# Graph-transformer layer: transposes, masks and scores of two thirds of the attention pair by pair in one TensorE array mode, ScalarE with fewer masks and more copies

## The reference, cut to what matters

```python
scores = einsum('ehd,ehd->eh', q[origin], k[destination]) * SCALE
ws = scores * edge_weights
e = exp(ws - segment_max(ws, origin)[origin])
att = e / (segment_sum(e, origin)[origin] + 1e-16)
values = segment_sum(att[:, :, None] * v[destination], origin)
values = (values @ W1 + b1) @ W2 + b2
```

## Time and profile before

| | us |
|---|---|
| median of 3 runs (1079.01 to 1079.73) | 1079.44 |
| profiled execution | 1079.38 |
| its span, first to last instruction | 1077.5 |
| around the span | 1.9 |
| PE busy in the span | 737.6 |
| VectorE (DVE) busy | 544.0 |
| ScalarE (ACT) busy | 397.4 |
| attention, first scores to the end | 673 to 1077.5 |

### The profile page before, as it was taken

How to read it: one execution, slowest core, us unless ns; L and a number is a source line. 1 busy time by engine, 2 the same in 40 slices (tenths; PEclk the granted TensorE clock), 3 DMA queues, 4 the chain that set the end, 5 groups by cost and what they waited for, 6 DMA issues and landing times.

```text
span 1077.5 us, 13741 instructions
## 1 busy us (share of the span) xinstructions
PE 737.6 (68%) x4498; PEld 436.4 (41%) x4537; DVE 544.0 (50%) x1269; ACT 397.4 (37%) x943; POOL 392.7 (36%) x401
## 2 busy tenths in 40 slices
PE   7744510494332211115999999999999999999996
PEld 4321100241001011003544454576766667767773
DVE  4601400482000110200532473888889999999998
ACT  2300001020000000001313020689989998877773
POOL 2677577477777776562572000000000000000002
PEclk9956655696555555556999999999999999999998
DMA  9788866536500000002400021444444444443323
GB/s 323 270 292 302 281 239 212 179 112 219 193 23 3 23 3 22 22 3 79 153 2 1 1 79 78 149 185 172 158 157 157 161 164 167 150 140 137 137 69 96
DMA packets 71115, 143.12 MB, mean 133 GB/s; under 512 B 22565, under 2 KB 57137, under 8 KB 67079
## 3 DMA queue, kind: packets, MB, share of 16 engines
q1 hardware_dynamic: 48884, 120.06, 30.7%
q10 hardware_dynamic: 8464, 15.84, 4.2%
q0 software_dynamic: 13696, 6.33, 3.1%
HBM read 77.47 MB, written 64.80 MB: 132 GB/s over the span
## 4 chain that ended last, share of the span: by engine, by line
PE 50%; another core or an unknown queue 20%; issue 20%; DVE 6%; ACT 2%; DMA 2%; ACTq 1%; DVEq 0%; POOLq 0%
PE bank L1092 11%; PE bank L1319 9%; PE bank L1364 7%; PE bank L1342 7%; PE bank L1077 6%; PE bank L1388 3%; PE bank L1326 2%; DVE AR L1841 1%; PE bank L1370 1%; DMA AR<-in_L_mix_bp_dram 1%; DVE QMN L1451 1%; DVE QMN L1450 1%; PE bank L1112 1%; DMA AR<-kv_rows,xd 1%
## 5 line engine op out<-in xcount | busy, mean ns | idle before, releaser
L630 POOL DMA_INDIRECT w_tab<-pay,idx x330 | 326.5, 989 | 160.0 <-issue 116.1
L1077 PE MATMUL bank<-AR 128*128 128x512 f32 (+1 forms) x288 | 130.9, 587 | 122.7 <-issue 102.8
L705 POOL DMA_INDIRECT AR<-kv_rows,xd x10 | 10.5, 1051 | 445.4 <-PE bank L1364 331.6
L1092 PE MATMUL bank<-AR 128*128 128x512 f32 (+1 forms) x240 | 128.6, 666 | 62.4 <-issue 62.4
L1077 PEld LDWEIGHTS bank<-AR 128*128 128x128 f32 x288 | 62.3, 222 | 180.3 <-issue 156.3
L1541 DVE TENSOR_TENSOR V<-bank,bias_row 128x512 f32<-128x512 f32 (+1 forms) x10 | 6.9, 691 | 250.0 <-remote 153.5
L912 ACT ACTIVATE AR<-AR,nmx 128x512 f32<-128x512 f32 (+1 forms) x180 | 118.5, 662 | 20.6 <-DVE nmx L1855 20.5
L1841 DVE CUSTOM_DVE_ANT_0 AR<-bank,AR,MX 128x512 f32<-128x512 f32 (+1 forms) x120 | 114.9, 986 | 8.6 <-remote 7.6
L1319 PE MATMUL bank<-KT,QT 64*128 64x512 f32 (+1 forms) x480 | 108.6, 568 | 4.0 <-ACT bank L920 3.7
L1092 PEld LDWEIGHTS bank<-AR 128*128 128x128 f32 (+1 forms) x240 | 48.3, 205 | 133.5 <-issue 133.0
L1364 PE MATMUL bank<-AR,V 128*64 128x128 f32 (+1 forms) x1520 | 101.9, 274 | 0.2 <-ACT AR L927 0.2
(11 more groups left out here) (272 smaller groups left out, 1013.2 us busy)
## 6 DMA issues: line engine op xcount, KB each, us to landing
w_tab<-ztile SPq DMA_DIRECT2D x20, 2280.0 KB
AR<-w_tab SPq DMA_DIRECT2D x20, 2048.0 KB, 7.4
AR<-w_tab SPq DMA_DIRECT2D x10, 1344.0 KB, 6.2
w_tab<-ztile SPq DMA_DIRECT2D x3, 1800.0 KB
w_tab<-pay,idx POOLq DMA_INDIRECT x330
w_tab<-ztile SPq DMA_DIRECT2D x2, 1700.0 KB
kv_rows<-AR ACTq DMA_DIRECT2D x9, 256.0 KB
kv_rows<-V ACTq DMA_DIRECT2D x9, 256.0 KB
```

The source lines that it names most:

```text
L630: pool.indirect_dma_start(out=w_tab, out_offset=bass.IndirectOffsetOnAxis(ap=idx[:, k, j:j + 1], axis=0), in_=pay[:, k % RING, j, :], in_o ...
L1077: last = mm(b[:, 0:n], w[:, k, m * P:(m + 1) * P], src_t(k), start=(k == 0), stop=(k == KC - 1))
L1092: last = mm(b[0:r, :], src_t(k)[:, 0:r], w[:, k, :], start=(k == 0), stop=(k == KC - 1))
```

## The change

In groups 0 and 1 and in the even steps of group 2 (`paired`), TensorE works pair by pair: scores of pair u, first half of its masks, first halves of the transposes of pair u-2, second half of the masks, second halves of the transposes. Masks and transposes are split by rows of the array, 64 at a time, head 0 in one half of the rows while head 1 is in the other, and then the other way round. Between first and second halves TensorE waits for its own first ones (`s_mh`, `s_th`). `factor`, `inverse` and the first `loser_k` are split the same way there. The order of `USES` follows. ScalarE lays only the masks of pair 2 (and in group 2 head 1 of pair 3) and copies head 1 of pairs 0 and 2, of pairs 0, 1 and 2, and of pair 2 in the three groups. ScalarE's and VectorE's orders in groups 0 and 1 are rewritten pair by pair. The values stay as they are, and so do the odd steps of group 2.

```diff
-ODD_ON_ACT = ((2,), (1, 2), ())
-OVER_MASK = (((3, 1), (1, 1), (2, 0), (2, 1)), ((3, 1), (1, 1), (2, 0), (2, 1)), ((2, 0), (2, 1), (3, 1), (0, 0), (1, 0)))
+ODD_ON_ACT = ((0, 2), (0, 1, 2), (2,))
+OVER_MASK = (((2, 0), (2, 1)), ((2, 0), (2, 1)), ((2, 0), (2, 1), (3, 1)))
...
+def paired(d):
+    return d < 4 * NT or (d < ND and d % 2 == 0)
+def half(j, n):
+    return slice(64 * j, min(64 * j + 64, n))
...
 for _d in range(ND + 4):
     _w, _q = _d // 2, _d % 2
+    if paired(_d):
+        USES += [("s", 2 * _d, 0), ("s", 2 * _d, 1)]
+        if _q == 1 and NT <= _w - 1:
+            USES += [("f", _w - 1)]
+        if _d:
+            USES += [("t", 2 * _d - 2, 0), ("t", 2 * _d - 2, 1)]
+        USES += [("s", 2 * _d + 1, 0), ("s", 2 * _d + 1, 1)]
+        if _q == 1 and _w + 1 == 2 * NT:
+            USES += [("l", _w + 1)]
+        if 2 * NT <= _w - 2:
+            USES += [("r", _w - 2)]
+        if _d:
+            USES += [("t", 2 * _d - 1, 0), ("t", 2 * _d - 1, 1)]
+        continue
...
 ...
+                if w < 2 * NT:
+                    if d:
+                        pairs(2 * d - 2)
+                    if q == 0 and NT <= w - 1:
+                        change(w - 1)
+                    if q == 0 and 2 <= w <= NT + 1:
+                        keep(w - 2)
+                    exps(2 * d)
+                    if q == 0:
+                        for u, hh in lay_order(d):
+                            lay_mask(u, hh)
...
+                    if d:
+                        pairs(2 * d - 1)
+                    exps(2 * d + 1)
...
 ...
+            def mask_half(u, part):
+                w, n = u // 4, GROUPS[u // 4 // NT][1]
+                bare = [hh for hh in range(2) if not laid(u, hh)]
+                if bare and part:
+                    pe.wait_ge(s_mh, mh.n)
...
+                for hh in bare:
+                    rows = half((hh + part) % 2, P)
+                    last = mm(use(("s", u, hh))[:, 0:n], identb[rows, :], pen[w % 2][rows, 0:n], start=False, stop=(part == 1))
...
+            def turn_halves(u, part):
+                g, r = u // 4 // NT, rows_of(u // 4 % NT)
+                bl = blocks(g)
+                if part == 0:
+                    for hh in range(2):
+                        pe.wait_ge(s_exp, 2 * u + hh + 1)
+                        free(pe, ("t", u, hh))
+                for i, (a, rws, _) in enumerate(bl):
+                    for hh in range(2):
+                        rows = half((hh + part) % 2, r)
+                        last = mm(use(("t", u, hh))[0:rws, i * P + rows.start:i * P + rows.stop], ws[g][u % 4][hh][rows, a:a + rws], ident[rows, rows],
+                                  start=(part == 0 and i == 0), stop=(part == 1 and i == len(bl) - 1), is_transpose=True)
...
+            def pair_step(d, i):
+                w, q = d // 2, d % 2
+                u, older = 2 * d + i, 2 * d - 2 + i
...
+                pair_scores(u)
+                mask_half(u, 0)
+                if fac:
+                    factor_half(w - 1, 0)
...
+                if inv:
+                    inverse_half(w - 2, 0)
+                if d:
+                    turn_halves(older, 0)
+                mask_half(u, 1)
+                pe.wait_ge(s_th, th.n)
+                if fac:
+                    factor_half(w - 1, 1)
...
+                if inv:
+                    inverse_half(w - 2, 1)
+                if d:
+                    turn_halves(older, 1)
...
 ...
+                if w < 2 * NT:
+                    if q == 0 and NT <= w - 1:
+                        change(w - 1)
+                    if q == 0 and NT <= w - 2:
+                        merged(w - 2)
+                    weighted(2 * d, 0)
+                    weighted(2 * d, 1)
+                    early = q == 1 and w + 1 == 2 * NT
+                    if early:
+                        rescaled(w - 1)
+                    if d:
+                        odd_of(2 * d - 2)
+                    shift_of(2 * d)
+                    weighted(2 * d + 1, 0)
+                    weighted(2 * d + 1, 1)
+                    if q == 1 and NT <= w - 1 and not early:
+                        rescaled(w - 1)
+                    shift_of(2 * d + 1)
+                    if q == 1:
+                        mask(w + 1)
...
+                    if d:
+                        odd_of(2 * d - 1)
+                    if q == 0 and NT <= w - 1:
+                        denominators(w - 1)
```

More of the change, by code:

```diff
@@ L94, in lay_order @@
     else:
-        order = ((0, 0), (0, 1), (1, 1)) if late else ((1, 1), (0, 0), (0, 1))
+        order = ((0, 0), (0, 1), (1, 1)) if late else ((0, 0), (0, 1))
     return [(2 * d + 2 + i, hh) for i, hh in order if d + 1 < ND and laid(2 * d + 2 + i, hh)]
@@ L993, in _ @@
                             lay_mask(u, hh)
-                    if late:
-                        pairs(2 * d - 1)
+                    pairs(2 * d - 1)
                     exps(2 * d)
@@ L1326, in scores, with pair_scores @@
                         mm(use(("s", u, hh))[:, 0:n], identb[:, :], pen[w % 2][:, 0:n], start=False, stop=True).then_inc(s_s[i], 1)
+            mh, th = Count(pe, s_mh), Count(pe, s_th)
+            def pair_scores(u):
+                w, p = u // 4, u % 4
+                g, c = w // NT, w % NT
+                d0, n = GROUPS[g]
+                over = [laid(u, hh) for hh in range(2)]
+                if g == 2 and p == 0:
+                    gone(pe, ("l", w))
+                if u in (1, 2):
+                    banks_left((2 * u - 2, 2 * u - 1))
+                for hh in range(2):
+                    if over[hh]:
+                        pe.wait_ge(s_laid, LAID_OF[u, hh] + 1)
+                    else:
+                        free(pe, ("s", u, hh))
+                for hh in range(2):
+                    last = mm(use(("s", u, hh))[:, 0:n], QT[64 * hh:64 * hh + 64, p, c * P:(c + 1) * P], KT[64 * hh:64 * hh + 64, p, d0:d0 + n],
+                              start=not over[hh], stop=over[hh], skip_group_check=over[hh])
+                    if over[hh]:
+                        last.then_inc(s_s[2 * (u % 2) + hh], 1)
@@ new lines, in factor_half @@
+            def factor_half(w, part):
+                if part == 0:
+                    pe.wait_ge(s_fo, w - NT + 1)
+                    free(pe, ("f", w))
+                rows = half(part, P)
+                for p in range(KC):
+                    last = mm(use(("f", w))[:, p * P + rows.start:p * P + rows.stop], fo[rows, p * P:(p + 1) * P], ident[rows, rows],
+                              start=(part == 0 and p == 0), stop=(part == 1 and p == KC - 1), is_transpose=True)
+                if part:
+                    last.then_inc(s_fp, 1)
+                else:
+                    th.inc(last)
@@ new lines, in inverse_half @@
+            def inverse_half(w, part):
+                if part == 0:
+                    pe.wait_ge(s_rb, w - 2 * NT + 1)
+                    free(pe, ("r", w))
+                rows = half(part, P)
+                for p in range(KC):
+                    last = mm(use(("r", w))[:, p * P + rows.start:p * P + rows.stop], te[rows, p * P:(p + 1) * P], ident[rows, rows],
+                              start=(part == 0 and p == 0), stop=(part == 1 and p == KC - 1), is_transpose=True)
+                if part:
+                    last.then_inc(s_rp, 1)
+                else:
+                    th.inc(last)
@@ new lines, in loser_half @@
+            def loser_half(w, part):
+                c = w - 2 * NT
+                if part == 0:
+                    pe.wait_ge(s_kvx[c % 3], 16 * (c // 3 + 1))
+                    free(pe, ("l", w))
+                rows = half(part, X)
+                for k in range(KC):
+                    last = mm(use(("l", w))[:, k * X + rows.start:k * X + rows.stop], KVx[c % 3][rows, k * P:(k + 1) * P], ident[rows, rows],
+                              start=(part == 0 and k == 0), stop=(part == 1 and k == KC - 1), is_transpose=True)
+                if part:
+                    last.then_inc(s_kxp, 1)
+                else:
+                    th.inc(last)
@@ L1415, in _ @@
                     ffn(w - 2)
-                if q == 1 and 2 * NT <= w + 1 < NW:
+                if q == 1 and 2 * NT <= w + 1 < NW and not paired(d):
                     loser_k(w + 1)
-                if 1 <= d <= ND:
+                if d <= ND and not paired(d):
                     transposes(d - 1)
```

53 lines of the change are left out of this document (38 added, 15 removed).

## The result

The changed kernel takes 1106.84 us (median of 4 runs, 1104.39 to 1109.63), the kernel before 1079.22 beside it: ratio **1.0263** [1.0232, 1.0294], slower.

What follows compares the result with a forecast made beforehand. TensorE was taken as the bound, with an order across three engines running just beside it. Group terms of +1.5, +12.5 and +5.9 us sum to +19.9 on 1079.38, so 1099 us, range 1074 to 1114.

Steps and rivals of the forecast that it cites:

- main case: Orders across engines and bank waits in all three groups outweigh TensorE's saving: +19.9 us, 1099 us, chance 64%.
- only group 0's chain holds: Rival: bank waits of groups 1 and 2 are covered by something misread; 1081 to 1086 us, chance 10%.
- Group 0: Even step 6.91 us by laid masks behind two exponentials, odd 5.6; tile 12.5 against 12.4, +1.5 us over ten tiles.
- Group 1: Laid masks, transposes' bank and `rescaled`'s bank hold the steps: tile 14.45 us against 13.0, +12.5 us in all.
- Group 2: Even steps: pair 3's transposes wait for the bank of pair 0's second scores, +0.74 us each, +5.9 us in all.
- The bounds: Ranges around each group's sum: -4 to +7 us in group 0, +6 to +17 in group 1, 0 to +9 in group 2.
- TensorE's own work: Group 0: scores, masks, half transposes, values and waits add up to 11.4 us a tile against 12.4.
- PE busy falls by 15 us or more: Sign over the whole kernel: TensorE's busy time falls that much while the span grows.
- Price of a round: Half transposes on TensorE: 0.06 us for two heads side by side, 0.24 for a group of four rounds.
- TensorE's wait for itself: Between first and second halves: 0.06 us behind a mask half, 0.31 where nothing is between, as in pair 2.
- the saving comes through: Rival: group 0 goes at 11.4 us, group 1 at 11.7 + 0.3; 1060 us, with half of it 1070; chance 17%.
- rival of halves that don't overlap: Rival: two heads' half transposes run one after the other, four rounds 0.48 us; 19 us more, 1118 us; chance 9%.

Runs made afterwards that it cites:

- e1: Changed kernel with ScalarE laying pair 2's masks ahead of pair 0's exponentials in groups 0 and 1: 722.96 us, 1.0154 of the kernel before.
- e2: Changed kernel with `rescaled` moved ahead of the second pair's products on VectorE in all of group 1: 732.16 us, 1.0283 of the kernel before.
- e3: Changed kernel with group 2 put back as in the kernel before, its laid masks too: 731.3 us, 1.028 of the kernel before.
- e7: Changed kernel with the edits of e1, e2 and e3, and VectorE's next-tile mask behind an odd step's first shift: 1077.7 us, 0.9981 of the kernel before.
- e10: e7 with, in group 1, VectorE's denominators moved to the odd step and all transposed heads copied by ScalarE: 1069.7 us, 0.9953 of the kernel before.

## Why the prediction was right, and where it was off

- **The main case held**, in its mechanism and its sign. The three waits it named are there: laid masks behind two exponentials in groups 0 and 1 (1.0 us each), `rescaled` whose bank is the next tile's (0.8), the transposes of pair 3 behind pair 0's bank in group 2 (0.65). e1, e2 and e3 take away one each: 14.2, 5.4 and 4.9 us of the stage, 24.5 in sum, and all three together 25.5 (430.1 to 404.6), all but 0.2 of what the change had cost. The rival in which only group 0's chain holds falls with that.
- **Group 0 was mis-sized**: said +1.5 us, measured 5.5. The even step has 7.11 in place of 6.91. The product starts 0.07 later. From there to the end of the shift it is 2.39 us (751.43 to 753.82) where the sum had 2.22: it had each operation of VectorE start 1.02 behind the one before, but the shift needs the maxima of its own pair and starts only 0.11 behind the *end* of the second product (752.44 + 1.10 to 753.65). In the earlier trace rows the shift stands behind a product that it doesn't need, and starts before that one ends (product at 750.86, 1.10 long; shift at 751.87). The laid masks took 0.05 less. The odd step has 0.04 more. The tile was to be 12.52 and is 12.76, and the tile before was 12.38 by the steps' medians rather than 12.4: 0.38 a tile, 3.4 us in nine. The other 2 us are nearly all in the first tile, 12.83 us against 11.04, which the sum took as one like the others. Before, eight products of the branch ahead of it (`last_mix`) stood in front of the first transposes and covered the exponentials; in the changed kernel they stand behind them, and TensorE waits 1.43 and 0.30 us (before, then after):

```profile
678.85 3.60 PE L1332 MATMUL bank<-QMN 128*98 128x512 f32 x8
682.28 1.91 PE L1342 MATMUL bank<-ident,AR 128*128 128x128 f32 x16
```

```profile
678.39 0.47 PE L1411 MATMUL bank<-ident,AR 64*128 64x64 f32 x8 [1.43 <-ACT AR L938]
...
681.74 3.67 PE L1491 MATMUL bank<-QMN 128*98 128x512 f32 x8
```

- **Group 1**: tile 14.45 said, 14.56 by the medians; +12.5 said, +13.1 measured. Its even step misses by the same term: 2.34 stands for two products of 1.10 and a shift of 0.18, which are 2.38 (and the terms as written add up to 7.03, not 7.05), and it took 2.50. **Group 2**: even step +0.74 said, +0.81 measured; +5.9 and +7.1, of which eight even steps are 6.5.
- **The bounds** of the three groups add up to +2 and +33, so 1081 to 1112; the prediction says that its terms span 1088 to 1111. The measured time lies within both.
- **TensorE's own work** was said to fall by 1 us a tile in group 0. That step failed: it set 11.4 us of added-up work against 12.4 of a tile's length, while the earlier trace rows had only 11.98 busy in it; and the work is some 11.7 by e7, where next to nothing else binds. The 0.3 missing are no one price: most of it is in pair 1, which takes 2.14 us in e7 (757.15 to 759.29) where its terms with the change of mode are 1.97. Its scores last 0.92 and not 0.86, and its transposes start 0.31 behind the first mask half and not 0.22; by the bank list they wait for VectorE's first product of the step, which ends 0.16 before them. Pairs 2 and 3 take 0.04 and 0.05 more. So the sign "PE busy falls by 15 us or more" did not come: it is 737.6 and 737.0. The forecast of the time didn't hang on it.
- **Price of a round**: 0.06 us was taken against the 0.107 that the Trainium skill (TensorE: Matmul & The Clock Gate, LDWEIGHTS) gives for such a load. Four rounds, in two halves of the array at once, took 0.26 to 0.29 us with what stands around them, so 0.07 at most, where the page would have 0.43 us for four: the trace decides against it here.
- **TensorE's wait for itself** where nothing is between: 0.31 said. In the odd step of after two rounds of four and that wait last 0.80 us (757.45 to 758.25); 0.80 less 0.26 and 0.29 leaves 0.25.
- **The rival "the saving comes through"** fell for this kernel. In e7 group 0 goes by TensorE's own work, as that rival had it, but at 11.72 us a tile and not 11.4, so 3.9 us under the kernel before and not 10. Its group 1, VectorE's 11.7 + 0.3, is what no order reached: e10 has 12.57, by TensorE. The rival of halves that don't overlap fell, too: four rounds would last 0.48 us.
- **A version that beats both** is e10, though only by half a per cent: 0.9953 of the kernel before [0.9934, 0.9971], its stage 6.2 us shorter. It is 32 us of stage under the changed kernel with the same TensorE work in groups 0 and 1. How much of the gain the pairing has over a kernel before with as well tuned queues was not tried.

## What to carry to other kernels

When three engines are all nearly always busy (here 89 to 97% in a tile of group 0), price a change by the longest chain from step to step, with each queue's order written out and each bank's next user looked up, and only then by the work that it saves. A producer of something that a step waits for (a laid mask, a bank released) goes ahead of work that nobody waits for yet; that cost 25 us here and no engine was busier. An operation that needs the result of the one right ahead of it on its own engine does not follow it as closely as any other: look for a row with the same dependence before taking the price from a row without it. And compare added-up work with busy time, not with the length of a tile.

## What the runs showed of the hardware that was not expected

- The same kernel before takes 711 us on one chip and 1075 to 1081 on the others; the attention steps that can be compared are the same. The difference lies ahead of it: between 150 and 200 us the kernel before on the long chip runs nothing on TensorE and VectorE, at clock 0.50, while e1 on the short one keeps TensorE busy throughout (the windows of the two, in this order):

```profile
150.00:200.00 50.00, 0.00 (x0) 0.00 (x0) 0.00 (x0) 4.19 (x6) 32.99 (x34) 0.50 0.56 191
```

```profile
150.00:200.00 50.00, 50.00 (x179) 25.10 (x178) 19.71 (x42) 12.33 (x20) 38.42 (x39) 0.93 0.85 298
```

  Code and work of that part are the same in both kernels. GpSimd's scatter is not what is slower: its 330 operations are busy for 326.5 us in the long one and 333.0 in the short one, where the attention starts while it still runs. What holds the engines was not settled, and it is in each of the totals around 1080 us. The short front also makes that chip's ratios larger for the same number of microseconds.
